# Third spline convolution of a graph network: groups of eight nodes with one load of 256 sorted rows, two rows a partition

## The chip, the cores and the metric

The kernel runs on one NeuronCore of a Trainium2 chip. The metric is the device time of one execution in microseconds (us), the median of several runs without the profiler. Short names of the engines: PE is TensorE (PEld its weight loads), DVE is VectorE, ACT is ScalarE, POOL is GpSimd, and SP is SyncE, which only issues DMA transfers and waits.

## The reference, cut to what matters

A graph has 12,500 nodes with 32 features and 200,000 random edges, sorted by `dst`; `src` is random. Two layers run one after the other: a spline convolution network (first layer) and a graph attention layer (second). The first layer has three spline convolutions that sum into the node `row = src`. The third is the one that is changed:

```python
new_pseudo = jnp.clip(pseudo + t[col] - t[row], 0.0, 1.0)
basis2, idx2 = spline_basis(new_pseudo)              # 8 weights of 125 for each edge
return spline_conv(x, row, col, basis2, idx2, conv_w, conv_b)

def spline_conv(x, row, col, basis, idx, W, b):      # x: [N, 32], W: [125, 32, 32]
    z = jnp.einsum('ni,kio->nko', x, W).reshape(N * K, Fout)
    gathered = z[col[:, None] * K + idx]
    msg = jnp.einsum('es,eso->eo', basis, gathered)
    out = jax.ops.segment_sum(msg, row, num_segments=N)
    deg = jax.ops.segment_sum(jnp.ones_like(msg[:, 0]), row, num_segments=N)
    return out / jnp.maximum(deg, 1.0)[:, None] + b
```

The kernel turns the order round: for every node it first sums basis(edge) x features(col) over the node's edges, which gives a 125 x 32 matrix for each node, and multiplies that with W.

## The kernel before, in words

The program is a row of phases with a barrier between them: loading, counting (`count_and_prefix`), sorting the edges by `src` (`sort_edges`), a first convolution on ones, the hidden layer, the second convolution (`flow_conv` named `c2`, 64 features), the third convolution (`flow_conv` named `c3`, 32 features, `moved` given), a layer norm, and the attention.

After the sort the edges lie in DRAM in the order of their nodes (200,704 rows with the padding, 1,568 tiles of 128), in a table `rows` of 84 words each. Nodes are cut into 98 blocks of 128 (`NB`). A block is cut into 32 windows of 4 nodes (`WN`, `NW`), and half a block (16 windows, `GW2`, one value of `q`) is one item of work, called a half block from here on. There are 196 of them in each convolution. A window has some 64 edges on average (200,000 / 12,500 x 4), and always 128 consecutive sorted rows are loaded from the window's first row on; what belongs to a later window is masked off by `mark`. Were a window fuller than 128, the whole pass would be repeated; here it runs once.

In `flow_conv` five engines work side by side:

- POOL gathers the features of the other end of each edge: for each tile of 128 edges one indirect DMA (`gather_slot`, L961), for four tiles one store of the features into `rows` (`store_slot`, L968). 1,568 tiles are gathered in a phase, 16 in each turn of the loop. A finished slot counts `done` up.
- SP loads windows (`load_windows`). For a block it waits until `done` has reached `need` of the block (L1012); for each half block it waits until DVE has used up the tile `rin[:, q]` of the same half of the block before (L1017), reads 16 row numbers, and issues 16 loads of 128 rows of 40 words (L1022), each into its own window of `rin`, and one load of the nodes' shifts `trow` (L1026). `rin` is doubled over `q`.
- DVE (`body`) waits for the loads and for PE's use of the buffers (`loaded`, `summed`; L1110), makes `rel`, `pos`, `mark` (128 rows x 16 windows x 4 nodes), `tsel` and `tsrc` (the shift of the own node), the clipped `pos`, and eight pieces of `spread` = `mark` x features (L1084, each piece two windows: 2 x 32 x 4 values a partition). Before the seventh piece it waits for ACT's `sides` (L1144), then makes `hat`, `plane` and in two halves `basis` (L1100, 16 x 125 values).
- PE (`body`) does for each window one matmul of `basis` (128 rows x 125) with `spread` (128 rows x 128 columns) into a PSUM bank, two windows side by side in one of four banks (L1222). In float32 a matmul of the program is two instructions. After each two blocks it multiplies with W (`mix_blocks`, L1234).
- ACT copies each pair of windows out of PSUM (`take_sums`, L1321) and makes the hat functions of the next half block (`make_sides`, lines L663 to L668 of a helper). Its order is written out: the sides of half block m + 1 come behind the eight copies of half block m.

Sides of half block m + 1 thus stand behind the copies of m; `basis` of m + 1 behind its sides; the matmuls of m + 1 behind its `basis`:

```python
take_sums(i * 2, 0, 0)
make_sides(i * 2, 1)
take_sums(i * 2, 0, 1)
make_sides(i * 2 + 1, 0)
```

`c2` has no `moved`: no `sides`, 64 features, so that a window's matmul has 256 columns and a piece of `spread` 512 values a partition.

Of the kernel before, what the change touches and what calls it, by code (L numbers as in the profile page):

```python
# [13 lines left out]
P = 128  # L14
# [7 lines left out]
G = 8  # L22
# [33 lines left out]
SLOT_OF = (4, 4)  # L56
RWORDS = HID + KEEP


# [161 lines left out]
def count_and_prefix(nc, c, d, sem):  # L221
# [6 lines left out]
    with nc.Block() as block, ExitStack() as ctx:  # L228
# [12 lines left out]
        turned = ps("cnt_turned", [P, 512])  # L241
        off = sb("cnt_off", [NB, NW], I32)
        starts = sb("cnt_starts", [1, NB * NW], I32)
        tot_sb = sb("cnt_tot", [P, 2, NB])
# [10 lines left out]
        def _(dve):  # L255
# [50 lines left out]
            chain(dve.tensor_copy(off[:, :], first))  # L306
            dve.sem_inc(off_made, 1)

            chain(dve.tensor_copy(c.in_start[:, :], start[:, 0:NB]))
# [16 lines left out]
            for k in range(2):  # L326
                begin = start[0:1, 0:NB] if k else c.base[0:1, 0, :]
                chain(dve.tensor_copy(block_fill[:, 0:NB], begin))
                chain(dve.memset(block_fill[:, NB:NB + 1], float(EP)))
                if k == 0:  # L330
                    for w, slot in enumerate(SLOT_OF):
                        chain(dve.tensor_scalar(need[:, :], block_fill[:, 1:NB + 1], float(P + slot * P - 1), float(EP),
                                                ALU.add, ALU.min))
                        chain(dve.tensor_copy(c.need[:, w, :], need[:, :]))
                        chain(dve.tensor_scalar(c.need[:, w, :], c.need[:, w, :], (slot * P).bit_length() - 1, None,
                                                ALU.logical_shift_right))
                else:
# [12 lines left out]
                    for w, value in enumerate((AT_TURNS - 1, 1, AT_TURNS)):  # L350
                        chain(dve.memset(c.lag4_all[:, w:w + 1], value))
# [58 lines left out]
        def _(sp):  # L410
# [4 lines left out]
            sp.wait_ge(stored, 32)  # L415
            sp.sem_inc(act_c, 1)


def sort_edges(nc, c, d, sem):
# [21 lines left out]
    with nc.Block() as block, ExitStack() as ctx:  # L441
# [59 lines left out]
        def _(sp):  # L501
# [7 lines left out]
            sp.dma_start(d.rows[EP:EP + P, :], blank[:, :, :].rearrange("p t w -> p (t w)")[:, 0:RWORDS])\  # L509
                .then_inc(blank_stored, 16)  # L510
# [358 lines left out]
def flow_conv(nc, c, d, sem, name, turn, table, width, feats, outs, weight, conv_out, moved):  # L869
# [22 lines left out]
    cleared = sem(f"{name}_cleared")  # L892
    pieces = GW2 // 2
    slot = SLOT_OF[turn]
    tiles = RING * slot
    turns, slots = NT // tiles, NT // slot
    loads = 16 * (GW2 if moved is None else GW2 + 1)
    steps = 4 if moved is None else 9
# [9 lines left out]
    with nc.Block() as block, ExitStack() as ctx:  # L908
# [4 lines left out]
        rel = sb(f"{name}_rel", [P, GW2])  # L913
        mark = sb(f"{name}_mark", [P, 2, GW2, WN])
        plane = sb(f"{name}_plane", [P, 2, GW2, 5, 5])
        basis = sb(f"{name}_basis_sb", [P, 2, GW2, 25, 5])
        spread = sb(f"{name}_spread_sb", [P, 2, GW2, feats, WN])
        sums = sb(f"{name}_sums", [K, feats, 2 * P])
# [4 lines left out]
        stack = {2: c.stack2[:, :], 4: c.stack4[:, :]}[strips]  # L923
        offsets = Offsets(sb, sem, name, d.off[0].rearrange("(a w) -> a w", a=1), NB * NW, P)
        acc = [ps(f"{name}_acc{k}", [K, 512]) for k in range(BANKS)]
# [11 lines left out]
        if moved is not None:  # L937
            trow = sb(f"{name}_trow", [P, 2, GW2 * WN, 4])
            tsel = sb(f"{name}_tsel", [P, GW2, WN, 3])
# [59 lines left out]
        def _(sp):  # L999
# [9 lines left out]
            def load_windows(o, b):  # L1009
# [3 lines left out]
                for q in range(2):  # L1013

                    sp.wait_ge(spread_made, (o * NB + b) * (2 * pieces) + (q + 1) * pieces)
                    for half in range(2):
                        _, offs = nc.values_load_multi_w_load_instructions(  # L1017
                            offsets.now[0:1, bass.ds(b * NW + (q * 2 + half) * G, G)], engines=(sp.engine,),
                            min_val=0, max_val=EP,
                            skip_runtime_bounds_check_because="prefix sums of EP counts, kept under EP by a pass's step")  # L1020
                        for w in range(G):
                            sp.dma_start(rin[:, q, half * G + w, :],  # L1022
                                         d.rows[bass.ds(offs[w], P), first_word:first_word + words])\
                                .then_inc(loaded[q], 16)
                    if moved is not None:
                        sp.dma_start(trow[:, q, :, :].rearrange("p n k -> p (n k)"),  # L1026
                                     bc(moved[bass.ds(b * P + q * GW2 * WN, GW2 * WN), :]
                                        .rearrange("n k -> (n k)").unsqueeze(0), [P, GW2 * WN * 4]))\
                            .then_inc(loaded[q], 16)
# [13 lines left out]
        def _(dve):  # L1043
# [31 lines left out]
            def body(b, item, q):  # L1075
# [5 lines left out]
                def make_spread(*ks):  # L1081
                    for k in ks:
                        w = slice(k * 2, k * 2 + 2)
                        dve.tensor_tensor(spread[:, q, w, :, :], bc(mark[:, q, w, :].unsqueeze(2), [P, 2, feats, WN]),  # L1084
                                          bc(rin[:, q, w, 0:feats].unsqueeze(3), [P, 2, feats, WN]), ALU.mult)\
                            .then_inc(spread_made, 1)
                        dve.wait_ge(spread_made, (m + 2) * pieces + k + 1)

                def make_mark():
                    dve.tensor_tensor(mark[:, q, :, :], bc(rel[:, :].unsqueeze(2), [P, GW2, WN]),  # L1090
                                      c.window_ramp[:, 2 * q:2 * q + 2, :, :].rearrange("p a g r -> p (a g) r"),
                                      ALU.is_equal).then_inc(seq, 1)
# [19 lines left out]
                if moved is None:  # L1112
# [14 lines left out]
                after_step(3)  # L1127
                dve.tensor_tensor(tsel[:, :, :, :].rearrange("p g r k -> p (g r) k"),
                                  bc(mark[:, q, :, :].rearrange("p g r -> p (g r)").unsqueeze(2), [P, GW2 * WN, 3]),
                                  trow[:, q, :, 0:3], ALU.mult).then_inc(seq, 1)  # L1130
                make_spread(0)
# [47 lines left out]
        def _(pe):  # L1179
# [32 lines left out]
            def body(b, item, q):  # L1212
                m = item * 2 + q
                for w in range(GW2):
                    pp = q * pieces + w // 2
                    if w % G == 0:
# [56 lines left out]
        def _(act):  # L1273
# [41 lines left out]
            with act.Fori(0, n) as o:  # L1315
                def take_sums(b, v, q):
                    item = o * NB + b
                    for pp in range(q * pieces, (q + 1) * pieces):
                        act.wait_ge(summed, item * (2 * pieces) + 2 * pieces + pp + 1)
                        at = v * P + pp * 2 * WN  # L1320
                        act.activation(  # L1321
                            sums[:, :, at:at + 2 * WN].rearrange("p f (k n) -> p k f n", n=WN),
                            acc[pp % BANKS][:, 0:pair].rearrange("p (k f n) -> p k f n", k=2, n=WN), ACT.Copy)\
                            .then_inc(taken, 1)
# [667 lines left out]
```

## Time and profile before

| | us |
|---|---|
| time, median of 3 runs | 11165.09 (11158.27 to 11210.48) |
| span of the profiled execution | 12528.6 |
| PE busy in it | 6505.4 (52%) |
| DVE busy | 7716.2 (62%) |
| POOL busy | 7476.5 (60%) |
| ACT busy | 2933.1 (23%) |

The profiled execution took 12528.6 us from its first to its last instruction; no other time of it is known. It is 12% longer than the median of the runs without the profiler. Stages and durations below are those of the profiled execution. The third convolution lies in it from 6669 us (its first DMA) to 9630 us (its last result).

### The profile page before, as it was taken

Reading aid. Unit: us, or ns where it says so; the run is one execution under the profiler, and the core shown is the slowest. Engines: PE = TensorE matmul, PEld = TensorE weight load, DVE = VectorE, ACT = ScalarE, POOL = GpSimd, SP = SyncE. Lnnn points to the kernel's source line nnn. Section 1 sums busy time; section 2 is a strip of 40 time slices with the busy share of each in tenths; the row PEclk is TensorE's granted clock in tenths of the full one; section 3 lists DMA queues with packets and bytes.
Section 4 is the critical chain, followed back from the end, with each engine's and each line's share of the span. In section 5 each row is a group of like instructions: output and inputs, shape, how many; then the busy total and the mean of one; then the engine's idle time right before and its main releaser. Section 6 shows DMA issues by size and latency. Waiting matters only on the chain. (4 is left out here: it accounts for less than half of the span.)

```text
span 12528.6 us, 178083 instructions
## 1 busy us (share of the span) xinstructions
PE 6505.4 (52%) x38968; PEld 5397.9 (43%) x38968; DVE 7716.2 (62%) x17239; ACT 2933.1 (23%) x8407; POOL 7476.5 (60%) x7456
## 2 busy tenths in 40 slices
PE   3466666666475799999994444545555100000000
PEld 2355555555475677777764434434454100000000
DVE  9844444444498676666664444544576267777777
ACT  0011111111132344344432222322343000000001
POOL 5155555655200888888886888888800566666663
PEclk9966666666698999999997667766777555555555
DMA  1210000000733444444443333333322212221221
GB/s 41 65 36 2 2 2 2 2 2 2 14 41 50 93 93 94 92 94 95 92 93 49 50 51 53 54 50 52 54 42 34 35 49 50 51 50 48 51 54 40
DMA packets 1788557, 605.09 MB, mean 48 GB/s; under 512 B 1595943, under 2 KB 1729575, under 8 KB 1788260
## 3 DMA queue, kind: packets, MB, share of 16 engines
q1 hardware_dynamic: 1078132, 311.05, 12.8%
q0 software_dynamic: 255648, 274.30, 10.7%
q10 hardware_dynamic: 454736, 19.28, 3.0%
q8 instruction: 15, 0.25, 0.0%
q14 instruction: 26, 0.21, 0.0%
HBM read 430.75 MB, written 172.95 MB: 48 GB/s over the span
## 5 line engine op out<-in xcount | busy, mean ns | idle before, releaser
L1222 PE MATMUL c_acc<-c_spread_sb,c_basis_sb 128*125 128x256 f32 (+1 forms) x12544 | 2599.2, 376 | 1502.8 <-issue 655.0
L1222 PEld LDWEIGHTS c_acc<-c_spread_sb,c_basis_sb 128*125 128x125 f32 x12544 | 2266.5, 231 | 1803.5 <-issue 1536.3
L1614 POOL DMA_INDIRECT at_ring<-gat_table,at_place x1568 | 1585.7, 1011 | 1188.5 <-issue 1188.5
L609 POOL DMA_INDIRECT rec<-rk_rec,rk_place x1568 | 1619.3, 1033 | 1110.1 <-DVE rk_place L497 620.7
L1321 ACT ACTIVATE c_sums<-c_acc 125x512 f32<-125x512 f32 (+1 forms) x3136 | 1489.3, 490 | 2258.7 <-PE c_acc L1222 1298.6
L961 POOL DMA_INDIRECT c_ring<-hid_table,c_at x1568 | 1707.1, 1089 | 478.9 <-issue 443.2
L961 POOL DMA_INDIRECT c_ring<-feat_table,c_at x1568 | 1602.7, 1022 | 478.1 <-issue 462.9
L1084 DVE TENSOR_TENSOR c_spread_sb<-c_mark,c_rin 128x512 f32<-128x512 f32 (+1 forms) x3136 | 1745.2, 557 | 60.3
L1871 PE MATMUL gr_hps<-ident,gr_hs 128*32 128x128 f32 x98 | 29.8, 408 | 2473.7 <-issue 2066.3
L492 DVE CUSTOM_DVE_ANT_0 rk_junk_l<-rk_look_ps,rk_hi 128x98 bf16<-128x98 f32 x1568 | 402.2, 257 | 1324.1 <-remote 821.1
L1234 PE MATMUL c_mix<-c_sums,c_w 125*64 125x256 f32 (+1 forms) x9408 | 1037.3, 401 | 187.6 <-issue 133.8
L554 PE MATMUL rk_look_ps<-rk_table,rk_lo_t 128*128 128x98 f32 x3136 | 908.7, 425 | 379.5 <-DVE rk_before L492 327.4
L1871 PEld LDWEIGHTS gr_hps<-ident,gr_hs 128*32 128x32 f32 x98 | 6.4, 109 | 2488.1 <-issue 2078.1
L554 PEld LDWEIGHTS rk_look_ps<-rk_table,rk_lo_t 128*128 128x128 f32 x3136 | 705.4, 292 | 503.3 <-DVE rk_before L492 404.2
L1783 DVE TENSOR_REDUCE at_sums<-at_prod 128x128 f32<-128x5248 f32 x98 | 873.3, 8911 | 24.0 <-issue 14.1
L1234 PEld LDWEIGHTS c_mix<-c_sums,c_w 125*64 125x64 f32 (+1 forms) x9408 | 627.4, 132 | 559.2 <-issue 304.0
L530 PE MATMUL rk_rows_ps<-ident,rk_cols 128*128 128x128 f32 x3152 | 771.1, 390 | 4.7 <-ACT rk_cols L564 4.5
L1110 DVE TENSOR_SCALAR c_rel<-c_rin,first 128x16 f32<-128x16 f32 x392 | 103.3, 264 | 1014.6 <-DMA c_rin<-rows 434.9
L587 ACT ACTIVATE rk_table<-rk_run_ps 128x98 f32<-128x98 f32 x784 | 196.2, 250 | 2173.9 <-PE rk_run_ps L549 1208.1
L530 PEld LDWEIGHTS rk_rows_ps<-ident,rk_cols 128*128 128x128 f32 x3152 | 664.9, 292 | 6.4 <-ACT rk_cols L564 6.4
L1144 DVE SCALAR_TENSOR_TENSOR c_hat<-c_hat,c_sides 128x96 f32<-128x96 f32 x196 | 52.5, 268 | 985.3 <-issue 785.6
L487 DVE SCALAR_TENSOR_TENSOR rk_junk<-rk_rows_ps,src_f,rk_earlier 128x128 bf16<-128x128 f32 (+1 forms) x1568 | 647.2, 413 | 2.0 <-PE rk_rows_ps L530 2.0
(356 smaller groups left out, 10126.9 us busy)
## 6 DMA issues: line engine op xcount, KB each, us to landing
c_rin<-rows SPq DMA_DIRECT2D x3136, 42.0 KB
c_rin<-rows SPq DMA_DIRECT2D x3136, 20.0 KB
rows<-c_ring POOLq DMA_DIRECT2D x392, 128.0 KB
rows<-rk_blank SPq DMA_DIRECT2D x112, 252.0 KB
rows<-c_ring POOLq DMA_DIRECT2D x392, 72.0 KB
rows<-at_ring SPq DMA_DIRECT2D x196, 144.0 KB
rec<-rk_rec,rk_place POOLq DMA_INDIRECT x1568
c_ring<-hid_table,c_at POOLq DMA_INDIRECT x1568
```

What stands on the lines that cost most here:

```text
L487: dve.scalar_tensor_tensor(junk[:, u, j // 2, odd:2 * odd + 1, :], rows[:, u, j - odd:j + 1, :], c.src[:, bass.ds(g * G + j, 1)], earlier[ ...
L492: dve.tensor_tensor_reduce(junk_l[:, u, j, :], look[:, j % 2, 0:NB], hi_hot[:, u, j, :], 1.0, 0.0, ALU.mult, ALU.add, before[:, u, j:j + 1 ...
L530: last = pe.matmul(rows[:, u, j, :], bc(cols[:, u, j:j + 1], [P, P]), c.ident[:, :], start=True, stop=True)
L554: pe.matmul(look[:, j % 2, 0:NB], lo_t[:, u, j, :], table[:, k % 2, :], start=True, stop=True).then_inc(looked, 1)
L609: pool.indirect_dma_start(out=d.rec, out_offset=bass.IndirectOffsetOnAxis(ap=place[:, u, j:j + 1], axis=0), in_=rec[:, u, j, :], in_offset ...
L961: pool.indirect_dma_start(out=ring[:, u, j, :], out_offset=None, in_=table, in_offset=bass.IndirectOffsetOnAxis(ap=at[:, h, u, j:j + 1], a ...
L1084: dve.tensor_tensor(spread[:, q, w, :, :], bc(mark[:, q, w, :].unsqueeze(2), [P, 2, feats, WN]), bc(rin[:, q, w, 0:feats].unsqueeze(3), [P ...
L1222: last = pe.matmul(acc[pp % BANKS][:, (w % 2) * WN * feats:(w % 2 + 1) * WN * feats], basis[:, q, w, :, :].rearrange("p a b -> p (a b)"), ...
L1234: last = pe.matmul(mix[k * outs:(k + 1) * outs, 0:2 * P], wsb[:, f, :], sums[:, f, :], start=(i_f == 0), stop=(i_f == each - 1))
L1321: act.activation(sums[:, :, at:at + 2 * WN].rearrange("p f (k n) -> p k f n", n=WN), acc[pp % BANKS][:, 0:pair].rearrange("p (k f n) -> p ...
L1614: pool.indirect_dma_start(out=ring[:, u, j, :], out_offset=None, in_=d.gat_table, in_offset=bass.IndirectOffsetOnAxis(ap=place[:, u, j:j + ...
L1783: dve.tensor_reduce(sums[:, v, :], prod[:, v, :, :, :].rearrange("p s h f -> p (h f) s"), X, ALU.add)\
```

## The change

A group is now 8 nodes in the third convolution (`deep = DEEP = 2`, `wide = WN * deep = 8`); the second keeps windows of 4 (`deep = 1`). A half block has 8 groups instead of 16 windows. One load brings 256 consecutive rows, rows 2p and 2p + 1 to partition p, and so fills two of the 16 places of `rin`. `mark` has 8 columns for each place instead of 4, a piece of `spread` 2 x 32 x 8 values, and a matmul 256 columns instead of 128; the two matmuls of a group add up in one PSUM bank (`start` on the first, `stop` on the second). There are still 16 matmuls, 8 pieces, 8 copies out of PSUM and 2 halves of `basis` in a half block. `tsel` is made in two instructions. The row numbers of the groups are kept in an array of their own (`off_wide`, `d.off[1]`), written by one more store in the counting phase; `need` of the third convolution lies 128 rows further on, and the blank rows behind the table are 256 instead of 128.

```diff
+DEEP = 2
...
+            wide = turned[0:NB, 0:P].rearrange("p (w n) -> p w n", n=WN * DEEP)[:, :, 0]
+            chain(dve.tensor_copy(off_wide[:, :], wide))
+            dve.sem_inc(off_made, 1)
...
-                        chain(dve.tensor_scalar(need[:, :], block_fill[:, 1:NB + 1], float(P + slot * P - 1), float(EP),
+                        chain(dve.tensor_scalar(need[:, :], block_fill[:, 1:NB + 1], float((1 + w * (DEEP - 1)) * P + slot * P - 1), float(EP),
...
+            sp.wait_ge(off_made, 2)
+            sp.dma_start(d.off[1][0:NB * NW // DEEP].rearrange("(b w) -> b w", w=NW // DEEP), off_wide[:, :])\
+                .then_inc(stored, 16)
+            sp.wait_ge(stored, 48)
...
+    deep = 1 if moved is None else DEEP
+    wide = WN * deep
+    groups = GW2 // deep
...
-        mark = sb(f"{name}_mark", [P, 2, GW2, WN])
+        mark = sb(f"{name}_mark", [P, 2, GW2, wide])
...
-        spread = sb(f"{name}_spread_sb", [P, 2, GW2, feats, WN])
+        spread = sb(f"{name}_spread_sb", [P, 2, GW2, feats, wide])
...
-                    for half in range(2):
+                    for half in range(groups // G):
...
                         for w in range(G):
-                            sp.dma_start(rin[:, q, half * G + w, :],
-                                         d.rows[bass.ds(offs[w], P), first_word:first_word + words])\
-                                .then_inc(loaded[q], 16)
+                            at_tile = (half * G + w) * deep
+                            sp.dma_start(rin[:, q, at_tile:at_tile + deep, :],
+                                         d.rows[bass.ds(offs[w], P * deep), first_word:first_word + words]
+                                         .rearrange("(p j) w -> p j w", j=deep)).then_inc(loaded[q], 16)
...
-                dve.tensor_tensor(tsel[:, :, :, :].rearrange("p g r k -> p (g r) k"),
-                                  bc(mark[:, q, :, :].rearrange("p g r -> p (g r)").unsqueeze(2), [P, GW2 * WN, 3]),
-                                  trow[:, q, :, 0:3], ALU.mult).then_inc(seq, 1)
+                for j in range(deep):
+                    last = dve.tensor_tensor(tsel[:, :, :, :].rearrange("p (w j) r k -> p j w r k", j=deep)[:, j, :, :, :],
+                                             bc(mark[:, q, :, :].rearrange("p (w j) r -> p j w r", j=deep)[:, j, :, :]
+                                                .unsqueeze(3), [P, groups, wide, 3]),
+                                             trow[:, q, :, 0:3].rearrange("p (w r) k -> p w r k", r=wide), ALU.mult)
+                last.then_inc(seq, 1)
...
-                    last = pe.matmul(acc[pp % BANKS][:, (w % 2) * WN * feats:(w % 2 + 1) * WN * feats],
+                    last = pe.matmul(acc[pp % BANKS][:, side * wide * feats:(side + 1) * wide * feats],
                                      basis[:, q, w, :, :].rearrange("p a b -> p (a b)"),
-                                     spread[:, q, w, :, :].rearrange("p f n -> p (f n)"), start=True, stop=True)
+                                     spread[:, q, w, :, :].rearrange("p f n -> p (f n)"), start=(w % deep == 0),
+                                     stop=(w % deep == deep - 1))
```

## Rows read from the trace of the kernel before

**Rows 1.** The page, part 2: slices of 313 us, busy tenths, granted clock

```profile
PE   3466666666475799999994444545555100000000
POOL 5155555655200888888886888888800566666663
PEclk9966666666698999999997667766777555555555
```

**Rows 2.** Line L961, the gathers: ns min/median/max, first and last start in us

```profile
L961 POOL DMA_INDIRECT c_ring<-feat_table,c_at x1568: 941/948/1988, 6669.8 to 9086.6; - x196
```

**Rows 3.** Line L1026, one load of trow for each half block, in the same columns

```profile
L1026 SPq DMA_DIRECT2D c_trow<-move x196: 3/333/725, 6716.4 to 9606.5; - x196
```

**Rows 4.** Timeline of SP while POOL gathers: start, duration in us, what

```profile
7604.45 11.24 SPq L1022 DMA_DIRECT2D c_rin<-rows  x16
...
7620.47 14.05 SPq L1022 DMA_DIRECT2D c_rin<-rows  x16
```

**Rows 5.** Timeline of SP after POOL's last gather

```profile
9255.78 0.33 SPq L1026 DMA_DIRECT2D c_trow<-move  x1
9258.22 9.02 SPq L1022 DMA_DIRECT2D c_rin<-rows  x16
...
9277.70 0.33 SPq L1026 DMA_DIRECT2D c_trow<-move  x1
```

**Rows 6.** SP's waits from 6700 to 9080 us: total us, times, longest

```profile
SPq L1017 <- DVE c_spread_sb L1084: 212.0, 30, 21.5
```

**Rows 7.** Line L1022, SP's loads from 7500 to 8500 us: ns min/median/max

```profile
L1022 SPq DMA_DIRECT2D c_rin<-rows x994: 2/332/734, 7500.3 to 8494.3; - x199
```

**Rows 8.** Line L1022, the same from 9200 to 9600 us

```profile
L1022 SPq DMA_DIRECT2D c_rin<-rows x584: 332/333/346, 9200.1 to 9599.6; - x195
```

**Rows 9.** Timeline after POOL's last gather, one round: idle before in brackets

```profile
9262.91 0.59 ACT L663 ACTIVATE c_hat<-c_pos,knots 128x48 f32<-128x48 f32 x2
...
9267.83 5.42 PE L1222 MATMUL c_acc<-c_spread_sb,c_basis_sb 128*125 128x128 f32 x32 [5.24 <-DVE c_basis_sb L1100]
...
9273.70 0.61 ACT L663 ACTIVATE c_hat<-c_pos,knots 128x48 f32<-128x48 f32 x2
...
9278.69 3.75 PE L1222 MATMUL c_acc<-c_spread_sb,c_basis_sb 128*125 128x128 f32 x32 [0.17 <-issue]
```

**Rows 10.** Stretches: us, PE, PEld, DVE, ACT, POOL busy, granted clock, DMA

```profile
9268.00:9271.00 3.00, 3.00 (x15) 3.00 (x16) 1.19 (x4) 1.03 (x3) 0.00 (x0) 0.50 0.31 68
9272.00:9282.00 10.00, 9.22 (x112) 7.18 (x111) 7.74 (x19) 6.05 (x18) 0.00 (x0) 1.00 0.22 40
...
4099.00:4102.00 3.00, 3.00 (x8) 2.33 (x9) 2.86 (x5) 0.60 (x1) 2.39 (x3) 0.50 0.51 102
```

**Rows 11.** Groups of instructions by shape, whole span: busy us, mean ns

```profile
L1084 DVE TENSOR_TENSOR c_spread_sb<-c_mark,c_rin 128x512 f32<-128x512 f32 x1568 | 1085.8, 692 | 46.8
L1084 DVE TENSOR_TENSOR c_spread_sb<-c_mark,c_rin 128x256 f32<-128x256 f32 x1568 | 659.4, 421 | 13.5
L1128 DVE TENSOR_TENSOR c_tsel<-c_mark,c_trow 128x192 f32<-128x192 f32 x196 | 71.9, 367 | 6.7
L1133 DVE TENSOR_REDUCE c_tsrc<-c_tsel 128x48 f32<-128x192 f32 x196 | 69.2, 353 | 23.9
```

**Rows 12.** Timeline of PE at the start of the second convolution

```profile
4098.86 9.47 PE L1222 MATMUL c_acc<-c_spread_sb,c_basis_sb 128*125 128x256 f32 x32 [112.74 <-DVE c_spread_sb L1084]
4109.64 7.17 PE L1222 MATMUL c_acc<-c_spread_sb,c_basis_sb 128*125 128x256 f32 x32 [1.31 <-DVE c_spread_sb L1084]
4123.67 9.02 PE L1222 MATMUL c_acc<-c_spread_sb,c_basis_sb 128*125 128x256 f32 x32 [6.86 <-DVE c_spread_sb L1084]
```

**Rows 13.** Line L1303, a store of two rows a partition issued by ACT

```profile
L1303 ACTq DMA_DIRECT2D feat_table<-mt_step x49: 378/379/484, 4243.2 to 6664.4; - x49
```

**Rows 14.** Timeline of PE, first matmuls of the third convolution

```profile
6727.88 5.66 PE L1222 MATMUL c_acc<-c_spread_sb,c_basis_sb 128*125 128x128 f32 x32 [63.78 <-DVE c_basis_sb L1100]
```

**Rows 15.** Timeline at the end of the third convolution

```profile
9629.93 0.23 ACT L1332 ACTIVATE sum<-c_back 128x64 f32<-128x64 f32 x1 [0.72 <-PE c_back L1244]
```

More of the change, by code:

```diff
@@ L242, in count_and_prefix @@
         off = sb("cnt_off", [NB, NW], I32)
+        off_wide = sb("cnt_off_wide", [NB, NW // DEEP], I32)
         starts = sb("cnt_starts", [1, NB * NW], I32)
@@ L508, in _ @@
             sp.dma_start(d.rows4[EP:EP + P, :], blank[:, 0, :]).then_inc(blank_stored, 16)
-            sp.dma_start(d.rows[EP:EP + P, :], blank[:, :, :].rearrange("p t w -> p (t w)")[:, 0:RWORDS])\
+            sp.dma_start(d.rows[EP:EP + DEEP * P, :].rearrange("(p j) w -> p (j w)", j=DEEP),
+                         blank[:, :, :].rearrange("p t w -> p (t w)")[:, 0:DEEP * RWORDS])\
                 .then_inc(blank_stored, 16)
@@ L896, in flow_conv @@
     turns, slots = NT // tiles, NT // slot
-    loads = 16 * (GW2 if moved is None else GW2 + 1)
+    loads = 16 * (groups if moved is None else groups + 1)
     steps = 4 if moved is None else 9
@@ L923, in flow_conv @@
         stack = {2: c.stack2[:, :], 4: c.stack4[:, :]}[strips]
-        offsets = Offsets(sb, sem, name, d.off[0].rearrange("(a w) -> a w", a=1), NB * NW, P)
+        offsets = Offsets(sb, sem, name, d.off[turn][0:NB * NW // deep].rearrange("(a w) -> a w", a=1), NB * NW // deep,
+                          P * deep)
         acc = [ps(f"{name}_acc{k}", [K, 512]) for k in range(BANKS)]
@@ L937, in flow_conv @@
         if moved is not None:
-            trow = sb(f"{name}_trow", [P, 2, GW2 * WN, 4])
-            tsel = sb(f"{name}_tsel", [P, GW2, WN, 3])
+            trow = sb(f"{name}_trow", [P, 2, groups * wide, 4])
+            tsel = sb(f"{name}_tsel", [P, GW2, wide, 3])
             pos, tsrc = sb(f"{name}_pos", [P, 2, GW2, 3]), sb(f"{name}_tsrc", [P, GW2, 3])
@@ L1015, in load_windows @@
                     sp.wait_ge(spread_made, (o * NB + b) * (2 * pieces) + (q + 1) * pieces)
-                    for half in range(2):
+                    for half in range(groups // G):
                         _, offs = nc.values_load_multi_w_load_instructions(
-                            offsets.now[0:1, bass.ds(b * NW + (q * 2 + half) * G, G)], engines=(sp.engine,),
+                            offsets.now[0:1, bass.ds(b * (2 * groups) + q * groups + half * G, G)], engines=(sp.engine,),
                             min_val=0, max_val=EP,
@@ L1021, in load_windows @@
                         for w in range(G):
-                            sp.dma_start(rin[:, q, half * G + w, :],
-                                         d.rows[bass.ds(offs[w], P), first_word:first_word + words])\
-                                .then_inc(loaded[q], 16)
+                            at_tile = (half * G + w) * deep
+                            sp.dma_start(rin[:, q, at_tile:at_tile + deep, :],
+                                         d.rows[bass.ds(offs[w], P * deep), first_word:first_word + words]
+                                         .rearrange("(p j) w -> p j w", j=deep)).then_inc(loaded[q], 16)
                     if moved is not None:
                         sp.dma_start(trow[:, q, :, :].rearrange("p n k -> p (n k)"),
-                                     bc(moved[bass.ds(b * P + q * GW2 * WN, GW2 * WN), :]
-                                        .rearrange("n k -> (n k)").unsqueeze(0), [P, GW2 * WN * 4]))\
+                                     bc(moved[bass.ds(b * P + q * groups * wide, groups * wide), :]
+                                        .rearrange("n k -> (n k)").unsqueeze(0), [P, groups * wide * 4]))\
                             .then_inc(loaded[q], 16)
@@ L1083, in make_spread @@
                         w = slice(k * 2, k * 2 + 2)
-                        dve.tensor_tensor(spread[:, q, w, :, :], bc(mark[:, q, w, :].unsqueeze(2), [P, 2, feats, WN]),
-                                          bc(rin[:, q, w, 0:feats].unsqueeze(3), [P, 2, feats, WN]), ALU.mult)\
+                        dve.tensor_tensor(spread[:, q, w, :, :], bc(mark[:, q, w, :].unsqueeze(2), [P, 2, feats, wide]),
+                                          bc(rin[:, q, w, 0:feats].unsqueeze(3), [P, 2, feats, wide]), ALU.mult)\
                             .then_inc(spread_made, 1)
@@ L1089, in make_mark @@
                 def make_mark():
-                    dve.tensor_tensor(mark[:, q, :, :], bc(rel[:, :].unsqueeze(2), [P, GW2, WN]),
-                                      c.window_ramp[:, 2 * q:2 * q + 2, :, :].rearrange("p a g r -> p (a g) r"),
+                    shape = [P, groups, deep, wide]
+                    dve.tensor_tensor(mark[:, q, :, :].rearrange("p (w j) r -> p w j r", j=deep),
+                                      bc(rel[:, :].rearrange("p (w j) -> p w j", j=deep).unsqueeze(3), shape),
+                                      bc(c.ramp[:, q * groups * wide:(q + 1) * groups * wide]
+                                         .rearrange("p (w r) -> p w r", r=wide).unsqueeze(2), shape),
                                       ALU.is_equal).then_inc(seq, 1)
@@ L1215, in body @@
                     pp = q * pieces + w // 2
+                    side = 0 if deep > 1 else w % 2
                     if w % G == 0:
@@ L1321, in take_sums @@
                         act.activation(
-                            sums[:, :, at:at + 2 * WN].rearrange("p f (k n) -> p k f n", n=WN),
-                            acc[pp % BANKS][:, 0:pair].rearrange("p (k f n) -> p k f n", k=2, n=WN), ACT.Copy)\
+                            sums[:, :, at:at + 2 * WN].rearrange("p f (k n) -> p k f n", n=wide),
+                            acc[pp % BANKS][:, 0:pair].rearrange("p (k f n) -> p k f n", k=2 // deep, n=wide), ACT.Copy)\
                             .then_inc(taken, 1)
```

## The prediction

> **What bounds the kernel now.** The page's slices come first [rows 1]: the second convolution shows PE at 9 tenths with the clock near full, the third at 4 to 5, POOL at 8 in both, the clock at 6 to 7. So PE is not at a limit there, and the question is who paces whom. The line of POOL's gathers says that in the third convolution they run from 6669.8 to 9086.6 us [rows 2], with the last store close behind, say 9090, while the loads of `trow`, one for each half block, run on to 9606.5 [rows 3]: (9606.5 - 6716.4) / 195 = 14.8 us for a half block, against (9090 - 6670) / 196 = 12.3 us that POOL takes for the rows of one. POOL is not the last in this execution.
>
> SP's own timeline shows the pacer. While POOL gathers, 16 loads take 11.2 and 14.1 us [rows 4]; after POOL's end 16 loads take 9.0 us, and two half blocks pass from 9255.78 to 9277.70, 10.96 us each [rows 5]. SP hardly waits for anybody: 212 us in 30 waits for DVE in 2380 us [rows 6]. So in the execution that is drawn, issuing loads sets the stage. Halving the number of loads looks like the cure.
>
> Two things speak against taking that at its word. The first is how SP is slow. From 7500 to 8500 us the same DMA instruction is recorded with 2 ns at the least and 734 at the most [rows 7]; after the gathers it has its length to some ns, 332 to 346 [rows 8]. Nothing issues a DMA in 2 ns: records come in clumps, late. I read this as the writing of the records holding SP up while POOL's are also written. The trace alone cannot prove it, but the profiled execution is 12,528.6 - 11,165.1 = 1,363 us longer than the runs without the profiler, and that time must lie somewhere. The second is what stands behind the loads.
>
> **The round behind the loads.** ACT makes the sides of half block m + 1 only behind the copies of m, so sides, `basis`, matmuls and copies form a ring in which nothing overlaps. After POOL's end it can be measured [rows 9]: sides begin at 9262.91, PE starts at 9267.83, works 5.42 us to 9273.25, and the next sides begin at 9273.70. The round takes 10.79 us, 5.37 of it outside PE. PE's share has two values: 5.42 us when it had been idle for 5.24 us, with the clock granted at 0.50 (1.2 GHz) for the first microseconds, and 3.75 us when the multiplication with W had filled the gap, at 1.00 (2.4 GHz) [rows 9, 10]. That happens once in two blocks, one half block of four. The mean round is 5.37 + (3 x 5.42 + 3.75) / 4 = 10.4 us, just under SP's 10.96. So today the round is hidden by SP, and without the profiler, in my reading, by POOL's 12.3.
>
> **The change part by part.** *SP* issues 8 loads instead of 16. One load costs 9.02 / 16 = 0.56 us [rows 5]; a store with two rows a partition was issued in 378 ns against 333 for one row [rows 13, 8], so I add 0.05 us. Upper bound: a load of 256 rows costs as much as two of 128, and nothing is won; lower: 8 x 0.56. I take 8 x 0.61 = 4.9 us instead of 9.0, near the lower bound since the nearest row is 45 ns and not twice. SP then needs some 6.5 us for a half block, at the slower pace of [rows 4] some 10. The bytes and row pieces are the same.
>
> *PE* keeps 16 matmuls a half block, of 256 columns instead of 128. The second convolution has just that shape: 9.47 and 9.02 us after a pause of 113 and 6.9 us, 7.17 us after one of 1.3 [rows 12], the first of them again begins with the clock at 0.50 [rows 10]. In the new round PE pauses as long as before, so three of four half blocks cost (9.47 + 9.02) / 2 = 9.25 and one 7.17: 8.73 us instead of 5.00. All at the full clock it is 7.17, all from the pause 9.47.
>
> *DVE* keeps 8 pieces of `spread`, of 512 values: 692 ns instead of 421 [rows 11]. Two of them stand in the round, between sides and `basis`: +0.54 us. The other six, a second `tsel` (0.37), a wider `mark` and a longer sum for `tsrc` (bound: no more than `tsrc` again, 0.35, each) add at most 6 x 0.27 + 1.07 = 2.7 us to work that DVE does while PE multiplies, which PE's 8.7 us cover; were PE at 7.17, DVE would still be done with the clipped positions in time, since ahead of them stand three pieces (2.1 us), `tsel` (0.7), `tsrc` (at most 0.7) and five small steps (about 1), an estimate of 4.5 us from [rows 11].
>
> *ACT* copies the same 256 values a pair. *Counting*: one more small store and a copy on SP and DVE, beside DVE's chain that goes on behind it: nothing; without that cover about 2 us. `need` one tile later: at most one gather, 1.3 us, at the start. Blank rows: nothing.
>
> **The sum.** The round is 5.37 + 0.54 + 8.73 = 14.6 us; I use 14.5, since the last copies overlap a little. 196 rounds are 2842 us. Today's stage, from PE's first matmul at 6727.9 to the last result at 9629.9 [rows 14, 15], is 2902 us. Against the profiled execution itself the sum is 12,528.6 - 60 = 12,469: hardly anything. SP's relief is spent, because the round grows past POOL and almost to where SP was.
>
> The runs without the profiler, which are the metric, stand 1,363 us under it. There I let SP issue at 10.96 us a half block throughout, so that POOL's 2420 us set the stage: 9090, then the last block's loads (2 x 10.96) and 23 us from its last load to the result [rows 3, 15], and some 3 for landing: 9138 instead of 9630. That explains 492 of the 1,363 us. From PE's first matmul it is 2410 us. The new stage has none of that slack, as its round does not stand on SP: 2842. Difference +432 us, 11,165 + 432 = **11,597, say 11,600 us**.
>
> Bounds: all matmuls at the full clock, 13.0 us a round, 2552 us, +142: 11,307. All from the pause, 15.4 us: 3014. If POOL's gathers too are faster without the profiler, the old stage goes down to SP's 196 x 10.96 = 2148 us, and the difference up to 2842 - 2148 = +694: 11,859. I keep POOL's pace as recorded, as its gathers have a minimum of 941 and a median of 948 ns [rows 2], not the clumps of SP.
>
> **A rule against it.** The loads are 128 x 40 words, 20 KB. SP's rows say that their number paces the stage [rows 3 to 5]. The Trainium skill, "DMA: Bandwidth & Descriptors", section "Rules for kernel authors", says to coalesce many small transfers into one large one, because under 64 KB one mostly pays overhead. By that rule alone the stage would fall to POOL's pace, 492 us less, 10,673 us; the rows of the ring stand against that figure, and the first rival below is what they leave of it.
>
> **Rivals.** *The slow loads are real*, and in every run 16 loads take 11 to 14 us: for it speak SP's rows, against it the clumps and the 1,363 us. Then the old stage was 2902 us in the timed runs too, and the new one is 2842: 11,105 us, 0.5% faster; with PE at the full clock 2552, so 10,815; from the pause always, 3014, so 11,277. The rule of the Trainium skill named above ("DMA: Bandwidth & Descriptors", "Rules for kernel authors") leans to this rival. It decides if the old loads took longer than 14.5 us a half block in the runs that are timed.
>
> *POOL still sets the stage*: if the sides come earlier than I think, or the round is under 12.3 us without the profiler, the stage keeps its length and the time stays, 11,165 us (up to +25). Even at the full clock the ring's rows give 13.0, so it needs another 0.7 us; nothing in the rows offers it.
>
> *The change does not relieve SP* (a load of 256 rows costs double): 10.96 us is still under 14.5, so the forecast stays as it is.
>
> **Chances.** The forecast 0.78, the real slow loads 0.14, POOL still last 0.08. Half of the second is a gain beyond 0.5% (about the least that a measurement of this kernel can tell from no change), 0.07, and with some doubt of the ring 0.08; unchanged 0.11; slower 0.81. The range reaches from the rival's 11,105, rounded to 11,110, to the upper bound 11,859, rounded to 11,870; the forecast's own range is 11,300 to 11,870.
>
> **What would show it.** In the changed kernel's trace: 8 loads a half block in 4.9 to 7 us, SP waiting for DVE at L1017 of before; the gathers ending near 9090 and a tail of some 450 us behind them, or a little shorter than today's; from sides to sides 13 to 15.4 us, PE's 16 matmuls in 7.2 to 9.5 us, `spread` at 690 ns; ACT's idle time before its copies ended by PE. It is wrong if the round is shorter than the gathers' 12.3 us, if the tail behind the gathers vanishes, or if the span shrinks by hundreds of us while the timed runs shrink too: then the loads were slow in earnest.

## The result and the profile after

The change makes the kernel slower: 11,565.9 us (median, 11,563.5 to 11,569.4) against 11,161.7 in the runs of the kernel before, a recorded ratio of 1.0354 with a 95% interval of 1.0332 to 1.0376 (the two medians alone give 1.0362). By the medians that is 404 us; the forecast was +432 us on 11,165.

The page of the changed kernel, part 2, beside [rows 1]; one slice is 289 us here:

```profile
PE   3366666664767999998895666666666300000000
...
POOL 5177777772008888888867888888860277777773
PEclk9978887777988999999997888888888555555555
```

In the third convolution (slices 23 to 31) PE is up from 4 or 5 to 6. It still does not fill the slices, and POOL goes quiet in the last of them, with PE still at 6.

The lines of the gathers, of the `trow` loads (one for each half block) and of the last results in the changed kernel, in the columns of [rows 2]:

```profile
L975 POOL DMA_INDIRECT c_ring<-feat_table,c_at x1568: 940/972/1637, 6089.6 to 8609.3; - x196
...
L1041 SPq DMA_DIRECT2D c_trow<-move x196: 435/449/461, 6132.6 to 8953.5; - x196
...
L1355 ACT ACTIVATE sum<-c_back x49: 223/223/224, 6207.8 to 8993.0; 128x64 f32 x48, 128x64 f32<-128x64 f32 x1
```

A half block takes (8953.5 - 6132.6) / 195 = 14.47 us; 14.5 was forecast. The gathers are through at 8609 us, and the last result comes 384 us after the start of the last one: POOL does not set this stage.

The timeline of the changed kernel after POOL's last gather, one round, beside [rows 9]:

```profile
8710.74 0.59 ACT L673 ACTIVATE c_hat<-c_pos,knots 128x48 f32<-128x48 f32 x2
...
8712.48 0.27 DVE L1165 SCALAR_TENSOR_TENSOR c_hat<-c_hat,c_sides 128x96 f32<-128x96 f32 x1 [1.75 <-ACT c_hat L678]
...
8715.47 5.73 SPq L1037 DMA_DIRECT2D c_rin<-rows  x8
...
8716.20 8.81 PE L1244 MATMUL c_acc<-c_spread_sb,c_basis_sb 128*125 128x256 f32 x32 [5.78 <-DVE c_basis_sb L1118]
...
8725.33 0.59 ACT L673 ACTIVATE c_hat<-c_pos,knots 128x48 f32<-128x48 f32 x2
```

From sides to sides it is 14.59 us. PE begins 8716.20 - 8710.74 = 5.46 us behind the sides, 0.54 more than in [rows 9], then works 8.81. The loads (8 in 5.73 us) begin 0.73 us before PE's stretch and end inside it; of the waits in this round none is for them.

### The profile page after: what moved, and what is told of

Its sections match the earlier page's. It is cut to its first block and busy times, and to the rows that moved or that the text cites. A ratio compares the mean times of both kernels' runs of the same rounds, so it can differ in the third digit from the quotient of the medians.

```text
span 11561.8 us, 173187 instructions
## 1 busy us (share of the span) xinstructions
PE 6526.8 (56%) x38968; PEld 5364.9 (46%) x38968; DVE 8217.6 (71%) x17436; ACT 2997.4 (26%) x8407; POOL 7656.9 (66%) x7456
## 5 line engine op out<-in xcount | busy, mean ns | idle before, releaser
L1244 PE MATMUL c_acc<-c_spread_sb,c_basis_sb 128*125 128x256 f32 x12544 | 3204.3, 420 | 1277.3 <-DVE c_basis_sb L1118 932.7
L1244 PEld LDWEIGHTS c_acc<-c_spread_sb,c_basis_sb 128*125 128x125 f32 x12544 | 2605.0, 211 | 1837.4 <-issue 1346.2
L1099 DVE TENSOR_TENSOR c_spread_sb<-c_mark,c_rin 128x512 f32<-128x512 f32 x3136 | 2163.9, 690 | 60.1
L975 POOL DMA_INDIRECT c_ring<-feat_table,c_at x1568 | 1700.5, 1084 | 477.7 <-issue 443.9
L1257 PE MATMUL c_mix<-c_sums,c_w 125*64 125x256 f32 (+1 forms) x9408 | 867.0, 380 | 24.6 <-ACT c_sums L1344 24.6
L564 PE MATMUL rk_look_ps<-rk_table,rk_lo_t 128*128 128x98 f32 x3136 | 697.2, 355 | 2.8 <-DVE rk_before L501 2.5
L559 PE MATMUL rk_run_ps<-rk_hi,rk_lo 128*128 128x98 bf16 x1568 | 236.4, 241 | 790.3 <-ACT rk_table L597 790.3
L540 PE MATMUL rk_rows_ps<-ident,rk_cols 128*128 128x128 f32 x3152 | 654.0, 342 | 0.0
L982 POOL DMA_DIRECT2D rows<-c_ring x784 | 626.5, 799 | 15.2 <-DMA c_ring<-hid_table,c_at 10.3
L1797 DVE TENSOR_TENSOR at_prod<-at_weight,at_run 128x1280 f32<-128x1280 f32 x392 | 583.9, 1489 | 10.1
```

The lines of the kernel that those rows point to most:

```text
L540: last = pe.matmul(rows[:, u, j, :], bc(cols[:, u, j:j + 1], [P, P]), c.ident[:, :], start=True, stop=True)
L564: pe.matmul(look[:, j % 2, 0:NB], lo_t[:, u, j, :], table[:, k % 2, :], start=True, stop=True).then_inc(looked, 1)
L975: pool.indirect_dma_start(out=ring[:, u, j, :], out_offset=None, in_=table, in_offset=bass.IndirectOffsetOnAxis(ap=at[:, h, u, j:j + 1], a ...
L982: pool.dma_start(rows_v[:, bass.ds(t * tiles + u * slot, slot), :], ring[:, u, :, :]).then_inc(stored[u], 16)
L1244: last = pe.matmul(acc[pp % BANKS][:, side * wide * feats:(side + 1) * wide * feats], basis[:, q, w, :, :].rearrange("p a b -> p (a b)"), ...
L1257: last = pe.matmul(mix[k * outs:(k + 1) * outs, 0:2 * P], wsb[:, f, :], sums[:, f, :], start=(i_f == 0), stop=(i_f == each - 1))
```

## The experiments

**The kernel before, profiled again.** No edit.

> The kernel before, unchanged, for a second profile. The forecast's reading (the clumped records of SyncE held the loads up in the first profile; otherwise the gathers set the stage): in a profile without clumps, one half block every 12.3 us, the last result some 50 us after the last gather, the stage about 2410 us from TensorE's first matmul, the span near 11,160. Rival, the slow loads are real: 14.8 us a half block again, the stage 2900 us, with each DMA instruction's record near 333 ns or not.

Its span is 11,192.9 us, against 12,528.6 in the first profile of the same kernel; this run took 11,194.7 us, and the median of the timed runs beside it is 11,196.0. Its gathers, `trow` loads, last results, and SP's loads from 7500 to 8500 us:

```profile
L961 POOL DMA_INDIRECT c_ring<-feat_table,c_at x1568: 941/970/1973, 6116.7 to 8555.3; - x196
...
L1026 SPq DMA_DIRECT2D c_trow<-move x196: 332/333/379, 6163.1 to 8590.1; - x196
...
L1332 ACT ACTIVATE sum<-c_back x49: 224/224/226, 6223.2 to 8613.8; 128x64 f32 x48, 128x64 f32<-128x64 f32 x1
...
L1022 SPq DMA_DIRECT2D c_rin<-rows x1284: 332/333/505, 7500.2 to 8499.8; - x184
```

SP's waits there, from 6000 to 8560 us (total us, times, longest):

```profile
SPq L1012 <- POOLq L972: 313.8, 88, 32.5
...
SPq L1017 <- DVE c_spread_sb L1084: 5.3, 1, 5.3
```

The clumps of [rows 7] are gone, a half block takes 12.45 us instead of 14.8, and SP waits for POOL. The last result comes 51 us after the last store of features (8562.4); the forecast had put it 48 behind. POOL paces this execution, which is as long as the timed runs; leaving out gathers, below, tests the same without a reading of waits. Profiles below are compared with this one. Each ratio is against runs of the kernel before that were made beside it, on three chips, with medians of 11,196.0, 11,174.7 and 11,190.6 us.

**The ring broken up.** The changed kernel, with ACT making the next sides before its fifth copy instead of behind its eighth:

```diff
-                def take_sums(b, v, q):
+                def take_sums(b, v, q, following=None):
...
+                        if following is not None and pp == q * pieces + pieces // 2:
+                            make_sides(*following)
...
-                    take_sums(i * 2, 0, 0)
+                    take_sums(i * 2, 0, 0, (i * 2, 1))
...
-                    make_sides(i * 2, 1)
```

> The changed kernel with ScalarE's order changed: the sides of half block m + 1 stand behind the fourth of the eight copies of m instead of behind the eighth. Nothing else. Ring theory: the ring opens, VectorE can make the next basis while TensorE multiplies, and the stage falls from 14.5 us a half block to the gathers' 12.3: about 11,150 us, 415 less than the changed kernel, equal to before within 30 us. Rival, the wider matmuls or the VectorE work set the stage by their sum: 11,566 still. Rival, the load of 256 rows is slow to land: 11,566 still.

11,315.4 us, against 11,196.0 beside it: 1.0114 (1.0097 to 1.0131). Two thirds of the loss are given back, but not all. SP's waits from 6200 to 8200 us, and the gathers:

```profile
SPq L1026 <- POOLq L986: 733.5, 72, 12.5
SPq L1031 <- DVE c_spread_sb L1099: 5.0, 6, 1.7
```

```profile
L975 POOL DMA_INDIRECT c_ring<-feat_table,c_at x1568: 940/981/1675, 6084.1 to 8633.5; - x196
```

POOL paces again, as the ring theory says, at 13.0 us a half block. But it has become slower itself: from first to last gather 2549 us against 2439, +111. No theory on record expected that. The profile is that of the fastest of the five runs (11,264.7 us), so the others may have lost more there.

**Sixteen loads again.** The changed kernel, with each load of 256 rows as two DMAs.

```diff
...
-                            sp.dma_start(rin[:, q, at_tile:at_tile + deep, :],
+                            for j in range(deep):
+                                sp.dma_start(rin[:, q, at_tile + j, :],
...
-                                         .rearrange("(p j) w -> p j w", j=deep)).then_inc(loaded[q], 16)
+                                             .rearrange("(p j) w -> p j w", j=deep)[:, j, :]).then_inc(loaded[q], 16)
```

> The changed kernel with 16 loads a half block again: each load of 256 rows is cut into the even and the odd rows, 128 row pieces each, into the same places. Groups of eight, matmuls and spread as changed. Ring theory: SyncE needs some 11 us a half block under a round of 14.5, so 11,566 within 20 us: the halved number of loads is worth nothing here. Rival, loads pace the stage: slower than the changed kernel by up to 196 x (14.8 - 14.5) = 60 us or more.

1.0362 (1.0344 to 1.0379), 14.48 us a half block, as with eight loads. The halved number of loads is worth nothing here.

**The matmuls alone.** The kernel before, with every matmul of the third convolution issued twice.

```diff
-                    last = pe.matmul(acc[pp % BANKS][:, (w % 2) * WN * feats:(w % 2 + 1) * WN * feats],
+                    for again in range(1 if moved is None else 2):
+                        last = pe.matmul(acc[pp % BANKS][:, (w % 2) * WN * feats:(w % 2 + 1) * WN * feats],
...
```

> The kernel before with each matmul of the third convolution issued twice into the same place, the second over the first, so the result is as before: TensorE's share of the changed kernel without its wider spread, its loads or its groups. Ring theory: round 5.37 + 8.73 = 14.1 us against the gathers' 12.3, so the stage is 14.1 x 196 = 2764 us instead of 2410 and the time 11,160 + 350 = 11,510 us. Rival, TensorE is hidden: TensorE's 8.7 us and the multiplication with W's 1.2 are under 12.3, so 11,162 as before.

11,505.7 us, 1.0278 (1.0261 to 1.0295): 310 us more than the 11,196.0 beside it, where 350 was expected (that 11,510 was named is chance, since the runs beside it were 36 us slower than the 11,160 it starts from). PE's timeline shows a short and two longer stretches of a half block's matmuls:

```profile
7001.93 7.25 PE L1223 MATMUL c_acc<-c_spread_sb,c_basis_sb 128*125 128x128 f32 x64 [0.16 <-issue]
7014.42 9.09 PE L1223 MATMUL c_acc<-c_spread_sb,c_basis_sb 128*125 128x128 f32 x64 [5.25 <-DVE c_basis_sb L1100]
7028.68 8.79 PE L1223 MATMUL c_acc<-c_spread_sb,c_basis_sb 128*125 128x128 f32 x64 [5.17 <-DVE c_basis_sb L1100]
```

TensorE's longer stretch alone, with 16 loads and the short `spread`, makes 14.03 us a half block, 0.44 less than the change; two `spread` pieces in the round were priced at 0.54.

**Half of the gathers left out, in both kernels.** Two of every four gathers of the third convolution are not done; their places stay zero, so half of the edges count nothing there and the result is not the reference's.

```diff
+    fetches = slot if moved is None else slot // 2
...
-                for j in range(slot):
+                for j in range(fetches):
...
```

> The kernel before with two of every four gathers of the third convolution left out (the places that they would fill stay zero, so half of the edges count nothing there); stores, loads and everything behind them are as before. If the gathers set the stage in the timed runs (12.45 us a half block in the second profile of before), it now falls to SyncE's 10.96 us, 196 x 1.49 = 290 us less: about 10,905 us on a chip where before takes 11,196. If the loads or the ring set it, nothing changes.

> The changed kernel with the same half of the gathers left out. Ring theory: the round of 14.5 us stands on ScalarE, VectorE and TensorE alone, so the stage keeps its 14.5 us and the time stays within 20 us of the changed kernel's (1.035 x before). Rival, the gathers and the VectorE work slow each other and that is part of the loss: more than 50 us less.

The `trow` loads of the kernel before, and then of the changed one:

```profile
L1031 SPq DMA_DIRECT2D c_trow<-move x196: 332/333/353, 6138.8 to 8282.3; - x196
```

```profile
L1046 SPq DMA_DIRECT2D c_trow<-move x196: 435/449/463, 6118.6 to 8938.0; - x196
```

The kernel before falls to 0.9741 (0.9725 to 0.9757), 10.99 us a half block, with SP waiting for nobody from 6200 to 8200 us: SP's 10.96 of [rows 5] is the next limit. The changed one stays at 1.0341 (1.0324 to 1.0359) and 14.46 us. One is paced by POOL, the other not.

**Both: early sides and half of the gathers.** The edit of the early sides and that of the half gathers together, in the changed kernel.

> The changed kernel with early sides and half of the gathers of the third convolution left out (half of the edges count nothing there): what the change is worth where neither the ring nor the gathers set the stage. Then VectorE is next, with some 10.5 us of work in a half block and its waits, against SyncE's 10.99 us of the kernel before with half of the gathers (0.974 x before): I expect 10.7 to 11.5 us a half block, so 0.970 to 0.984 x before, no gain even there. If halving the loads pays once the others are out of the way, 9 to 10 us a half block and 0.94 to 0.957.

0.9828 (0.9812 to 0.9845), 11.53 us a half block: slower than the kernel before with the same gathers left out. From 7000 to 8000 us its engines look so (us, then busy PE, PEld, DVE, ACT, POOL, granted clock, DMA share, GB/s):

```profile
7000.00:8000.00 1000.00, 797.94 (x4312) 626.77 (x4313) 911.45 (x1736) 383.45 (x1254) 505.81 (x513) 0.92 0.35 58
```

With the ring and POOL out of the way DVE is 91% busy, and SP waits for it (626 us in 174 waits from 6200 to 8200). So the wider groups move the next limit to DVE and do not lower it.

**Why the gathers slow down.** First comes the kernel before, with six of the eight `spread` pieces made twice, so that DVE has more work in instructions as short as before:

```diff
+                        if moved is not None and k < 6:
+                            dve.tensor_tensor(spread[:, q, w, :, :], bc(mark[:, q, w, :].unsqueeze(2), [P, 2, feats, WN]),
...
...
+                            dve.wait_ge(once, m * 6 + k + 1)
```

> The kernel before with six of the eight pieces of spread of the third convolution made twice, one behind the other, the same values into the same place: 6 x 0.54 = 3.2 us more of VectorE in a half block, outside the part between sides and basis, about what the change adds there (2.8). Two theories of what the changed kernel with early sides still loses (its gathers took 2549 us, not 2439): a longer VectorE time slows the gathers, then here too their mean rises from 1040 to about 1090 ns and the time by 80 to 120 us; or the wider matmuls or the load of 256 rows slow them, then the gathers keep 1040 ns and the time stays within 20 us of before.

1.0001 (0.9991 to 1.0011): the first theory fell, for short instructions at least. The time is the one that the second theory named, but two earlier runs speak against its causes: with the doubled matmuls the gathers' mean is 1025 ns, and with sixteen loads it stays at 1084. Then comes the kernel with early sides, with each `spread` piece of the third convolution as two instructions of 256 values:

```diff
+                        for part in ([w] if moved is None else [slice(k * 2, k * 2 + 1), slice(k * 2 + 1, k * 2 + 2)]):
...
```

> The changed kernel with early sides, each piece of spread of the third convolution made by two instructions of 256 values instead of one of 512; VectorE works some 8 x 0.2 = 1.6 us longer in a half block. Theory: a gather that meets a VectorE instruction waits for its end, so one long instruction delays it more than two short ones: the gathers' mean falls from 1093 ns towards 1040, their stage from 2549 to some 2460 us, the time by up to 80 us, less where VectorE itself becomes the last (some 12 us). Rival, the amount of VectorE work slows the gathers: mean 1093 or more, time the same or longer.

1.0045 (1.0028 to 1.0062), against 1.0114 with the long pieces. The groups of gathers (busy us, mean ns, idle before) of the kernel before, the changed one, the one with early sides, the one with `spread` twice, and the one with early sides and short pieces:

```profile
L961 POOL DMA_INDIRECT c_ring<-feat_table,c_at x1568 | 1630.8, 1040 | 478.1 <-issue 455.0 <-DMA rows<-c_ring 13.7 <-DMA c_ring<-feat_table,c_at 8.5
```

```profile
L975 POOL DMA_INDIRECT c_ring<-feat_table,c_at x1568 | 1700.5, 1084 | 477.7 <-issue 443.9 <-DMA rows<-c_ring 25.0 <-DMA c_ring<-feat_table,c_at 7.9
```

```profile
L975 POOL DMA_INDIRECT c_ring<-feat_table,c_at x1568 | 1713.6, 1093 | 477.8 <-issue 409.3 <-DMA rows<-c_ring 43.6 <-DMA c_ring<-feat_table,c_at 24.1
```

```profile
L962 POOL DMA_INDIRECT c_ring<-feat_table,c_at x1568 | 1630.1, 1040 | 478.0 <-issue 448.5 <-DMA rows<-c_ring 20.4 <-DMA c_ring<-feat_table,c_at 8.2
```

```profile
L975 POOL DMA_INDIRECT c_ring<-feat_table,c_at x1568 | 1677.9, 1070 | 477.9 <-issue 451.7 <-DMA rows<-c_ring 17.4 <-DMA c_ring<-feat_table,c_at 7.9
```

More DVE work in short instructions leaves the mean at 1040 ns. Cutting the long `spread` instructions in two takes 23 ns off. 53 ns x 1568 = 83 us of the 111 us that POOL lost with early sides are gathers that take longer. What the other 30 of the 53 ns come from was not taken apart.

The length of the pieces is not the whole cause, as the runs with half of the gathers show. The gathers of the changed kernel, and then of the one with early sides:

```profile
L977 POOL DMA_INDIRECT c_ring<-feat_table,c_at x784 | 843.4, 1076 | 241.3 <-issue 223.9 <-DMA rows<-c_ring 11.1 <-DMA c_ring<-feat_table,c_at 5.5
```

```profile
L977 POOL DMA_INDIRECT c_ring<-feat_table,c_at x784 | 908.1, 1158 | 248.1 <-issue 191.8 <-DMA rows<-c_ring 41.4 <-DMA c_ring<-feat_table,c_at 14.0
```

Both make the same long pieces, but the second a half block every 11.53 us instead of 14.46. So how densely the work follows counts as well. All engines but POOL work more densely in the second, so whose work it is stays open.

**POOL's own side.** Eight tiles for one store instead of four, `SLOT_OF = (4, 8)`, with early sides in the changed kernel, and in the kernel before:

```diff
-SLOT_OF = (4, 4)
+SLOT_OF = (4, 8)
```

> The changed kernel with early sides and with one store of eight tiles instead of four in the third convolution (SLOT_OF 4, 8). If a store costs GpSimd a fixed 0.8 us and some 0.25 us around it, 196 stores fewer are 200 us less of the gathers' stage, from 1.011 x before to about 0.995; if it goes by rows, nothing.

> The kernel before with one store of eight tiles instead of four in the third convolution, none of the change. If the gain of that step in the changed kernel with early sides (from 1.011 to 0.995 x before, 165 us of the gathers' stage) is GpSimd's alone, it comes here too: gathers' stage 2439 - 165 = 2275 us, 11.6 us a half block, still above SyncE's 10.99, so 0.985 x before. If SyncE's or the ring's pace is nearer than that, less: the least is 10.99 us a half block.

0.9953 (0.9936 to 0.9970), and 0.9873 (0.9857 to 0.9890), 11,052.9 us against 11,190.6 beside it: the fastest of those that do all the gathers, and it does without the change. In the kernel before the last gather starts 2296 us behind the first instead of 2439, and a half block takes 11.74 us.

## Why the prediction was right, point by point

*What bounds the kernel.* The step that mattered was to distrust SP's rows. The second profile has the same instruction at 332 to 505 ns and 1,336 us less span. Of these, 463 us lie between the first gather and the last result of the third convolution, where 492 were worked out; the others lie ahead of it (553) and behind it (320), which the forecast left open. The old stage, from PE's first matmul (6174.8) to the last result (8613.8), measured 2439 us; 2410 was worked out. Of the 29 us, 22 are slower gathers: 2439 us from first to last here, 2417 in [rows 2], with means of 1040 and 1022 ns. So POOL's pace as recorded was not quite that of the timed runs.

*The round.* The new stage runs from 6147.1 to 8993.0, 2846 us; forecast 2842. PE's mean stretch is 8.77 us (8.73 was used), but it is made up otherwise than forecast: of four half blocks one takes 7.17 us, two take 8.8 to 9.0 and one takes 10.1, beyond the 9.47 that was named as the most. That the mean fits so well is in part luck. Over the one of 10.06 us below the granted clock is 0.71, over the one of 8.81 in the round shown above 0.81; why they differ was not looked into. Four half blocks in a row, with the multiplication with W ahead of the last:

```profile
7497.65 8.81 PE L1244 MATMUL c_acc<-c_spread_sb,c_basis_sb 128*125 128x256 f32 x32 [5.78 <-DVE c_basis_sb L1118]
7512.17 10.06 PE L1244 MATMUL c_acc<-c_spread_sb,c_basis_sb 128*125 128x256 f32 x32 [5.71 <-DVE c_basis_sb L1118]
7528.01 8.98 PE L1244 MATMUL c_acc<-c_spread_sb,c_basis_sb 128*125 128x256 f32 x32 [5.78 <-DVE c_basis_sb L1118]
...
7542.72 7.17 PE L1244 MATMUL c_acc<-c_spread_sb,c_basis_sb 128*125 128x256 f32 x32 [0.46 <-DVE c_basis_sb L1118]
```

The longer ones begin with the clock granted at 0.50, 1.2 GHz, behind a pause of 5.7 us; the short one, behind 0.46 us, has it at 1.00, 2.4 GHz, as two windows of the changed kernel show (in the columns of [rows 10]):

```profile
7512.30:7515.30 3.00, 3.00 (x7) 2.34 (x8) 2.84 (x8) 0.38 (x1) 2.39 (x4) 0.50 0.46 66
...
7542.80:7545.80 3.00, 3.00 (x14) 2.63 (x15) 2.84 (x8) 0.96 (x3) 2.59 (x4) 1.00 0.49 67
```

The pause is what the ring costs PE twice, once as idle time and once as clock.

*The sum.* 2846 - 2439 = 407 us by the profiles and 404 in the timed runs, against 432: the old stage's 29 us and the new one's 4 make the difference. The round was added up to 14.64 us and set to 14.5 for an overlap that no row gave; with 14.64 the new stage would have been 2869 us. The spans of the two profiles differ by 369 us and not by 407, because that of the kernel before reached its first gather 27 us later (6116.7 against 6089.6) and took 10 us more behind the stage.

*SP.* The loads take 5.73 to 5.77 us, 0.72 each, where 0.61 was used: within the bounds (0.56 to 1.13), but the row of the two-row store was too far off. It does not matter, since SP waits for DVE from 6000 to 8900 us:

```profile
SPq L1031 <- DVE c_spread_sb L1099: 1224.8, 190, 8.5
```

The rule weighed in the forecast (the Trainium skill, "DMA: Bandwidth & Descriptors", "Rules for kernel authors": coalesce transfers) holds for what SP spends, 5.8 us instead of 9.0. It gave no time here, as the sixteen loads show.

*DVE.* `spread` takes 687 ns (692 forecast), and `tsrc` 670, within its bound of 0.7 us. That they stay hidden is shown by DVE waiting for ACT at L1165, 521.5 us in 159 waits from 6200 to 8500 us:

```profile
L1165 DVE SCALAR_TENSOR_TENSOR c_hat<-c_hat,c_sides 128x96 f32<-128x96 f32 x159 | 42.8, 269 | 521.5 <-ACT c_hat L678 521.5
```

*POOL.* The step that was missing: its pace was taken as untouched, and it lost 4% (1040 to 1084 ns). The ring hid that; the tail behind the gathers came out at 384 us instead of 450, as they ended later. A hint stood in the trace of before, where the second convolution, with 512-value pieces, has gathers of 1089 ns, though of a wider table.

*The rivals.* The slow loads were not real in the timed runs. POOL sets the new stage only once the ring is broken up. That the loads are not relieved did not come true (0.72 us a load, where this rival needs 1.13), and it would have made no difference, as the sixteen loads show.

## What to carry to other kernels

Before an engine is relieved, work out the round that stands behind it, with every engine that hands work to the next and gets it back: here the change freed the engine that issues loads and lengthened the one chain that could not overlap. Where a profile is far longer than the timed runs, look for instructions whose durations scatter where elsewhere they are steady, and profile again before believing who paces whom. And look first at the engine that sets the stage: halving POOL's stores gave 1.3%, where rebuilding the groups cost 3.5%.

## What the runs showed of the hardware that was not expected

Two profiles of one kernel differed by 1,336 us of span (12,528.6 and 11,192.9). In the first, SP's DMA instructions lasted 2 to 734 ns while POOL gathered; in the second at least 332. That records were written late is a reading; what made them so is open.

What slows POOL's gathers is shown in part. They averaged 1040 ns beside `spread` instructions of 421 ns, also when there were nearly twice as many, 1093 beside pieces of 686 ns, and 1070 when those were cut to 419. But with half of the gathers left out the mean went from 1076 to 1158 ns beside equally long pieces that followed more densely. The Trainium skill, "SBUF — State Buffer", section "Who interferes with whom", says that VectorE and GpSimd share a pair of ports under an exclusive lock, and that a VectorE instruction with two SBUF inputs contends with a GpSimd instruction that reads SBUF. The same section infers that a `tensor_tensor`, as `spread` is one, takes only the read side of the pair, while making DMA descriptors needs the write side. The slower gathers agree with the first sentence and would not be expected from the second alone; that nearly twice the short pieces cost nothing at all (1.0001) is more than the first leads one to expect, and no run here shows the lock itself.

A `trow` load, the same in both kernels, takes SP 449 ns to issue behind loads of two rows a partition and 333 behind loads of one row, also in the changed kernel with sixteen loads (332 to 371). Why was not looked into.
